# Routed experts of a Mamba and MoE kernel: each slot tile's first expert weights fetched from DRAM into a ring of three groups, in place of a copy picked out of SBUF by VectorE

## The reference

```
def _ffn(xn, rw, W1, W2):
    ms = jnp.mean(xn * xn, axis=-1, keepdims=True)
    h = xn * jax.lax.rsqrt(ms + RMS_EPS) * rw
    return jax.nn.silu(h @ W1) @ W2

gates = jax.nn.softmax(xf @ router_w, axis=-1)           # 8192 tokens, 14 experts
top_v, top_i = jax.lax.top_k(gates, 2)
masked = zeros.at[arange(N)[:, None], top_i].set(top_v)
masked = masked / (masked.sum(-1, keepdims=True) + EPS)
routed = jax.vmap(lambda rw_, W1_, W2_: _ffn(xf, rw_, W1_, W2_))(rms_w, w1, w2)
routed_out = jnp.einsum('end,ne->nd', routed, masked)
shared = the same _ffn for 2 shared experts, summed
return routed_out + shared
```

## Time and profile before

| what | us |
|---|---|
| runs | 765.46, 766.20, 766.67; median 766.2 |
| span of the profiled execution | 769.2 |
| first return of group 0 on POOL | 481.1 |
| return of group 22 begins | 659.5 |
| last return (group 35) begins | 749.34 |

### The profile page before, as it was taken

How to read it: one execution, slowest core, us unless ns; L and a number is a source line. 1 busy time by engine, 2 the same in 40 slices (tenths; PEclk the granted TensorE clock), 3 DMA queues, 4 the chain that set the end, 5 groups by cost and what they waited for, 6 DMA issues and landing times.

```text
span 769.2 us, 14716 instructions
## 1 busy us (share of the span) xinstructions
PE 651.3 (85%) x4299; PEld 554.7 (72%) x4299; DVE 596.1 (77%) x1744; ACT 444.7 (58%) x1225; POOL 501.3 (65%) x545
## 2 busy tenths in 40 slices
PE   5987798999999999999999997965988878767830
PEld 4765576788888888888888886854987768656720
DVE  4999999999999999999999864427447343698875
ACT  4885688867877876787787543411223111346445
POOL 1144565887797897888888776556655656566561
PEclk9999999999999999999999998878889889997865
DMA  8541111211221121111111055114222236536126
GB/s 305 193 138 42 43 43 41 64 57 55 62 64 62 60 62 50 63 64 60 59 50 62 22 167 192 45 55 101 80 80 77 76 80 172 168 100 205 60 80 218
DMA packets 62638, 70.76 MB, mean 92 GB/s; under 512 B 10335, under 2 KB 45285, under 8 KB 62304
## 3 DMA queue, kind: packets, MB, share of 16 engines
q1 hardware_dynamic: 41568, 47.70, 19.6%
q0 software_dynamic: 8608, 16.87, 6.5%
q10 hardware_dynamic: 12384, 5.26, 2.9%
HBM read 48.55 MB, written 23.01 MB: 93 GB/s over the span
## 4 chain that ended last, share of the span: by engine, by line
PE 60%; DVE 13%; issue 12%; ACT 7%; another core or an unknown queue 4%; ACTq 2%; DMA 1%; DVEq 0%; SPq 0%
PE bank L745 7%; PE bank L817 6%; PE bank L826 6%; PE bank L884 6%; PE bank L770 5%; PE bank L800 5%; DVE xbcT_area L1155 3%; PE bank L881 3%; PE bank L871 3%; PE bank L833 3%; PE bank L785 3%; PE bank L888 2%; DVE decay_area L1163 2%; ACT x L933 2%
## 5 line engine op out<-in xcount | busy, mean ns | idle before, releaser
L623 POOL DMA_INDIRECT returned<-xT,slots_in x141 | 142.1, 1008 | 107.6 <-DVE xT L1453 67.3
L669 POOL DMA_INDIRECT dispatched<-rows,row_u x128 | 143.7, 1123 | 33.9 <-issue 31.8
L745 PE MATMUL bank<-xT 128*128 128x128 f32 x564 | 92.0, 316 | 43.4 <-issue 24.9
L1155 DVE SCALAR_TENSOR_TENSOR xbcT_area<-raw,conv_w,xbcT_area 128x512 f32<-128x512 f32 x162 | 123.9, 766 | 2.9 <-ACT xbcT_area L999 2.9
L745 PEld LDWEIGHTS bank<-xT 128*128 128x128 f32 x564 | 82.7, 226 | 50.7 <-issue 42.4
L944 ACT ACTIVATE raw<-bank 128x512 f32<-128x512 f32 (+1 forms) x71 | 39.8, 590 | 126.9 <-remote 61.5
L661 POOL TENSOR_TENSOR state_kept<-state,whole 128x256 f32<-128x256 f32 x56 | 72.1, 1288 | 59.0 <-DVE state L1181 49.1
L1453 DVE COPY xT<-bank 128x512 f32<-128x512 f32 (+1 forms) x36 | 24.3, 676 | 90.5 <-remote 72.8
L770 PE MATMUL bank<-xbcT_area,raw 128*128 x564 | 83.4, 308 | 4.7 <-issue 4.6
L1163 DVE TENSOR_TENSOR_SCAN decay_area<-decay_area,ident_heads 128x512 f32<-128x512 f32 x64 | 85.0, 1329 | 0.0
L770 PEld LDWEIGHTS bank<-xbcT_area,raw 128*128 128x128 f32 x564 | 79.6, 224 | 7.0 <-issue 7.0
(11 more groups left out here) (228 smaller groups left out, 1497.0 us busy)
## 6 DMA issues: line engine op xcount, KB each, us to landing
decay_area<-decay_rows SPq DMA_DIRECT2D x64, 256.0 KB
slots_in<-dispatched ACTq DMA_DIRECT2D x77, 64.5 KB
hid<-returned SPq DMA_DIRECT2D x18, 256.0 KB
slots_in<-dispatched SPq DMA_DIRECT2D x64, 64.5 KB
xT<-xT_dram SPq DMA_DIRECT2D x8, 512.0 KB, 7.9
x<-x_dram SPq DMA_DIRECT2D x8, 512.0 KB, 7.8
out_dram<-x SPq DMA_DIRECT2D x16, 256.0 KB
xT<-returned SPq DMA_DIRECT2D x14, 256.0 KB
```

The lines of the kernel that those rows point to most:

```text
L623: e.indirect_dma_start(returned, bass.IndirectOffsetOnAxis(ap=slots_in[sb_][:, n, D:ROW].bitcast(U32), axis=0), slots_out[b][:, n * P:(n + ...
L669: e.indirect_dma_start(dispatched, bass.IndirectOffsetOnAxis(ap=row_u[t % 2][:, m:m + 1], axis=0), rows[t % 3][:, k, c4, :], None).then_in ...
L745: mm = e.matmul(bank[:, off:off + P], w1_now[b][:, k * P:(k + 1) * P], slotsT[gr % len(slotsT)][:, n % 4 * P:(n % 4 + 1) * P], start=True, ...
L1155: e.scalar_tensor_tensor(o, r[:, n:n + W], conv_w[:, k, TAPS - 1 - n:TAPS - n], o, ALU.mult, ALU.add).then_inc(S["conv"])
```

## The change

`w1_routed` and the picks go. SP fetches, for each of the 141 slot tiles, the 128 x 256 block of its expert from the weights in DRAM (rows of 1 KB, 128 KB each) into `w1_now`, a ring of three groups that lies in the same area. The multiplication by `rms_w` moves to the turned slots: in place of one copy of 128 x 512, DVE has four `tensor_scalar` of 128 x 128 from PSUM to `slotsT`, each with the expert's column of `rms_w`, and each releases its own tile. The experts' numbers come as packed words, four to a word of 16 bits: one read of 12 registers (groups 0 to 11) and one of 24 (the others) on SP, PE and DVE; every tile's expert is a shift and a mask of such a register. For that, three steps are added to each of the two tables on DVE, and the words go from SBUF to DRAM and back as one row, the early ones on ACT's queue, the late ones on SP's. The late part of the tables (`run(later)`) starts one step of the loop earlier.

```
-            experts = []
+            packed = []
-                if gr == 1:
-                    on.wait_ge("mix", NC)
-                    e.dma_start(w1_routed, w1_v[:, 0:NR]).then_inc(S["w1r_loaded"], 16)
+            def load_w1(gr):
+                b = gr % W1_GROUPS
+                on.wait_ge("mix", NC)
+                if gr >= W1_GROUPS:
+                    on.wait_ge("routed_hidden", pairs_of(gr - W1_GROUPS)[-1] + 1)
+                for n in slot_tiles(gr):
+                    expert = expert_of(on, ET.SP, packed, gr, n % 4)
+                    e.dma_start(w1_now[:, b, n % 4, :], w1_v[:, bass.ds(expert, 1), :].rearrange("p o f -> p (o f)")).then_inc(S[f"w1_now{b}"], 16)
...
+            def expert_of(on, engine, packed, gr, j):
+            if gr in (0, EARLY_GROUPS) and j == 0:
+                row, n = (packed_row_early, 2 * TPE) if gr == 0 else (packed_row_late, 2 * TP)
+                on.wait_ge("packed_early" if gr == 0 else "packed_late", 16)
+                packed[:] = regs_of(engine, row, 0, n, 16 ** 4 - 1)
+            word = packed[gr if gr < EARLY_GROUPS else gr - EARLY_GROUPS]
+            return nc.s_assert_within((word >> 4 * j) & 15, 0, NR - 1, ...)
...
+                    e.dma_start(packed_late_d, packed_late).then_inc(S["packed_late_out"], 16)
+                    on.wait_ge("packed_late_out", 16)
+                    e.dma_start(packed_row_late, packed_late_d.rearrange("a b -> (a b)").unsqueeze(0)).then_inc(S["packed_late"], 16)
+                if gr >= W1_GROUPS + W1_LEAD:
+                    load_w1(gr - W1_LEAD)
                 if gr < LOADED_BY_ACT:
                     slots_free(on, gr)
                     if gr % 2 == 0:
                         first_rows = rows_of(ET.SP, gr)
                     load_slots(e, gr, first_rows)
+                if gr < W1_GROUPS:
+                    load_w1(gr)
...
             def routed_hidden(n2):
+                on.wait_ge(f"w1_now{gr % W1_GROUPS}", 16 * tiles_upto(gr, W1_GROUPS))
-                    on.wait_ge("w1_picked", n + 1)
-                    on.wait_ge("slots_turned", gr + 1)
+                    on.wait_ge("slots_turned", n + 1)
...
             def turned(gr):
-                e.tensor_copy(slotsT[gr % len(slotsT)][:, cols], dve_ring.bank("slotsT", gr)[:, cols]).then_inc(S["slots_turned"])
-            def pick_w1(gr):
-                if gr % 2 == 0:
-                    experts[:] = experts_of(on, ET.DVE, gr)
-                    e.tensor_scalar(w1_now[n % len(w1_now)], w1_routed[:, bass.ds(experts[n % 8], 1), :].rearrange("p o f -> p (o f)"), rms_w[:, bass.ds(experts[n % 8], 1)], None, ALU.mult).then_inc(S["w1_picked"])
+                    expert = expert_of(on, ET.DVE, packed, gr, n % 4)
+                    e.tensor_scalar(slotsT[gr % len(slotsT)][:, cols], dve_ring.bank("slotsT", gr)[:, cols], rms_w[:, bass.ds(expert, 1)], None, ALU.mult).then_inc(S["slots_turned"])
```

More of the change, by code:

```diff
@@ L342, in mamba_moe @@
         slotsT = [carve(W) for _ in range(3)]
-        w1_now = [carve(HB * P) for _ in range(8)]
         gexp = carve(NC * NR).rearrange("p (c r) -> p c r", c=NC)
@@ L374, in mamba_moe @@
         rows_a, full_a, base_a, end_a, row_base_a = (carve(NR) for _ in range(5))
-        t_expert_a, t_row_a = (carve(8)[0:TPE, :] for _ in range(2))
+        t_expert_a, t_row_a, in_places_a = (carve(8)[0:TPE, :] for _ in range(3))
         carve, _ = carver(x_third[:].rearrange("p n i -> p (n i)"))
@@ L379, in mamba_moe @@
         seg_sum = carve(SEGS)
-        in_any, t_segment, t_wrap, t_row = (carve(8)[0:TP, :] for _ in range(4))
+        in_any, t_segment, t_wrap, t_row, in_places = (carve(8)[0:TP, :] for _ in range(5))
         lower = y_carried[:, 0:NR * NR].rearrange("p (a b) -> p a b", a=NR)
@@ L427, in regs_of @@
             return vals
[L429 to L435, removed]
+        def expert_of(on, engine, packed, gr, j):
[4 more added lines that the diff above has]
+            word = packed[gr if gr < EARLY_GROUPS else gr - EARLY_GROUPS]
+            return nc.s_assert_within((word >> 4 * j) & 15, 0, NR - 1, skip_runtime_bounds_check_because="worked out from counts")
         def slots_free(on, gr):
@@ L550, in sync_program @@
                     pick(m)
+            for gr in range(GROUPS - W1_LEAD, GROUPS):
+                load_w1(gr)
             stored = 0
@@ L766, in routed_group @@
                     n2, j = n // 2, n % 4
+                    expert = expert_of(on, ET.PE, packed, gr, j)
                     on.wait_ge("routed_silu", n2 + 1)
@@ L1315, in early_table @@
                 yield
+                step(e.scalar_tensor_tensor(by_place(in_places_a), by_place(t_expert_a), float(NR - 1), places[0:TPE], ALU.min, ALU.mult))
+                yield
+                on.wait_ge("early_table", 24)
+                step(e.tensor_reduce(t_row_a[:, 0:2], by_place(in_places_a), AX.X, ALU.add))
+                yield
+                on.wait_ge("early_table", 25)
+                step(e.tensor_copy(packed_early, t_row_a[:, 0:2]))
+                yield
                 step(e.tensor_scalar(seg_row[:, 0], early_of[:], float(P), None, ALU.mult))
@@ L1392, in tables @@
                 assert experts_made == TABLE_EXPERTS, experts_made
+                after(experts_made)
+                placed = step(e.tensor_tensor(by_place(in_places), by_place(expert_late[:]), places[:], ALU.mult))
+                after(placed)
+                words = step(e.tensor_reduce(t_row[:, 0:2], by_place(in_places), AX.X, ALU.add))
+                after(words)
+                packed_made = step(e.tensor_copy(packed_late, t_row[:, 0:2]))
+                assert packed_made == TABLE_PACKED, packed_made
                 after(inside)
@@ L1399, in tables @@
                 after(rows_in)
+                after(packed_made)
                 row = step(e.tensor_reduce(t_row, is_in, AX.X, ALU.add))
```

61 lines of the change are left out of this document (35 added, 26 removed).

## The result

The changed kernel takes 781.1 us (median of 4 runs, 778.96 to 782.29) against 766.4 us before on the same chip: ratio 1.019, interval 1.016 to 1.022, 14.7 us slower. The forecast was 763 us with a range of 749 to 774. The profiled execution of the changed kernel has a span of 778.2 us, 9.0 us over that of before. A time is about 2 us above its span (780.22 us for the span of 778.2), so the profiled execution of the kernel before, with its span of 769.2, was more than 4 us slower than the median of its runs, not 3.0. Comparisons of stages between these two traces therefore understate the loss by 5.7 us in all (14.7 less 9.0).

The account below looks back on a forecast made before the run. Bounds: POOL's runs of indirect DMAs, with PE's slow single matmuls, in groups 12 to 22; DVE's work in groups 22 to 33. Terms -5.5 - 1 + 3 = -3.5 us: span 765.7, median 763 us, range 749 to 774.

Parts of the forecast that it names:

- The start: Ahead of group 1, SP must have the packed words before loading its slots: +3 us, ends 0 and +6.
- SP's queue later: SP in later groups: eight DMAs and a read, about 4.5 us against a pace of 6.5; cost 0.
- Picks out, scaled turns in: DVE in the tail (groups 22 to 33): 0.60 us saved a group, 7.2 at best; -5.5 us taken.
- There DVE is nearly full with the token sums and norms, so DVE's own work decides: Tail, groups 22 to 33: DVE's work sets the pace, a pair of groups taking 13.6 us.
- TENSOR_LOADs: 18 eight-register reads go on each of DVE and PE: -1 us, ends 0 and -3.6.
- The rival in which the stutters go with the reads: PE's slow single matmuls behind POOL's long runs, groups 2 to 22, go: -25 us, about 741; chance 0.12.
- a rival of +8 to +12 at 0.22: SP falls behind at over 0.8 us a DMA, first weights late from group 7 or 8: 772; chance 0.22.
- Traffic: 18.5 MB more in about 270 us, 68 GB/s on top of 79: taken as nothing.

Follow-up runs that it names:

- r5: Kernel before with its turned copy split into four scaled turns, picks kept as multiplications by 1.0: 725.2 against 718.9 us, ratio 1.008.
- r7_after: Changed kernel, unchanged, on chip B (the kind where the kernel before takes 717 to 719 us): 732.9 against 717.1 us, ratio 1.021.
- r4: Changed kernel without first-weight loads after group 2, packed words kept, outputs not the reference's: 721.9 us, ratio 1.006 against the kernel before.
- r15: r12_mended2 without first-weight loads after group 2, outputs not the reference's, on chip B: ratio 0.9965 against the kernel before.
- r17: r12_mended2 once more, on chip B: 718.3 against 718.1 us for the kernel before, ratio 1.000.
- r19: r15 once more, beside r17 (no first-weight loads after group 2, outputs not the reference's): ratio 0.9966 against the kernel before.
- r6_before: Kernel before, unchanged, profiled on chip B: 718.0 us (one execution).
- r8: Kernel before with the picks moved from DVE to ACT: 725.5 against 717.1 us, ratio 1.010.
- r13: Kernel before with late packed words on PE and DVE, their row 64 bytes into its area: 719.1 against 718.4 us, ratio 1.000.
- r18: Changed kernel with experts of groups 0 to 11 by eight-register reads, late packed words kept, on chip B: 723.2 against 718.1 us, ratio 1.007.
- r2: Changed kernel with experts by eight-register reads everywhere, no packed words: 722.4 against 718.9 us for the kernel before, ratio 1.007.
- r12_mended2: r18's kernel, SP reordered: second weights before group 1's first, late words behind group 12's slots, first weights from group 14 a group earlier; chip A, 1.007.
- r16: r12_mended2 with one DMA of four fixed experts a group for first weights, outputs not the reference's, on chip B: ratio 1.002.

## Why the prediction was wrong

Three terms failed: the start was priced at +3 and the early packed words alone cost 7 to 10 us; SP's queue later was priced at nothing and cost 5 us by its order and 2 by its loads on chip B; the tail was to give 5.5 us back and gave 1.8 on chip B and nothing on chip A.

**Picks out, scaled turns in.** The price of the operations was right: four scaled turns start to start take 1.04 us (r5) for 1.64 us of copy and picks. By the section "Why PSUM operands drop a tier" of "VectorE: DVE Perf Modes" in the Trainium skill an fp32 operand in PSUM holds a VectorE operation to the 1x mode. The trace agrees: half the elements out of PSUM took about as long as all of them within SBUF, 351 against 366 ns. The step that failed is "There DVE is nearly full with the token sums and norms, so DVE's own work decides". DVE had 6.5 us less to do in the tail on chip A and 6.0 on chip B. The tail shrank by 1.8 us on chip B (71.5 to 69.6) and grew by 2.0 us on chip A (659.55 to 736.81 before, 666.56 to 745.78 after). The freed time became waits before the copy of the result, 3.9 to 12.3 us on chip A, where no late weights stand in the tail; on chip B one late load of 3.45 us (r7_after) is part of it. Where no first weights are late in the tail (r4, r15, r17, r19, all on chip B) it is 2.0 to 3.6 us shorter than in r6_before, for 5.0 to 6.4 us less work on DVE. The granted clock of that stretch is higher too, 0.87 to 0.94 against 0.86, so not even all of this need be DVE's work; no run separates the two. A busy share of 85% was not enough to call DVE the bound. That the loop DVE, PE, ACT, PE, DVE is the bound instead is argued from these waits; r8 shows ACT's part in it. Term -5.5, measured +2.0 on the chip of the forecast, from one trace of each.

**TENSOR_LOADs.** Term -1, measured 0 for the 12 late reads (r13). The longer reads that came instead were forecast at 1.0 and 2.3 us and took 0.8 to 1.2 and 1.4 to 1.7 us in the changed kernel. The rival in which the stutters go with the reads is dead: the changed kernel has none of the 36 and keeps the stutters on A; the kernel before has all and no stutter on B.

**The start.** Term +3, ends 0 and +6. Measured +6.4 us at group 0 and 2.3 us more by group 3 on B; +5.1 at group 0 on A. With the early words gone the whole kernel wins 10 us on B (r7 against r18) and 7 on A. The mechanism was right and the term mis-sized. I priced the words' way by a DMA's landing, while the DMA out leaves only at 454.35 and the DMA in stands on ACT behind a step of the loop (5.5 us from out to in); group 1's slots were forecast 8 us late at the queue and were 11.4. The reason given for their slow issue before, two loads of 1.8 MB, does not hold either: the second left behind them, at 456.95. I also gave back part of the delay as absorbed by PE's idle time; on B all later groups carried it. The second weights, behind eight loads of first weights on SP, were seen in the order rows but not priced. They show once the early words are gone, with 2.50 us at the first `down` in r2; in the changed kernel itself PE waits 0 to 1.2 us there.

**SP's queue later.** The term was 0: "no cost in the steady state", with a rival of +8 to +12 at 0.22. On B groups 3 to 12 lose 6.3 us, the largest loss of one stage beside the start; on A PE waits 7.2 us for weights. The rival had the place right (groups 8 to 12, behind fills and late words). Its trigger, SP crawling at over 0.8 us a DMA, was seen on A (four loads in 4.3 us) but isn't needed: on B SP takes 0.6 us a load and the weights are late all the same, since their load waits in order behind slots, fills, the words' wait and, at group 24, the first pick of returned rows. The falls of the clock behind such waits, up to 3.0 us behind one, were not in the rival's price. What is shown for order rather than speed is r17 against r18: same loads, another order, 5 us.

**Traffic.** The term was 0; traffic and issues together cost 2 us once the order is mended (r17 against r19, 0.3%).

**The sum on chip B**, in ratios: changed kernel 1.021; early words away 1.007; SP's order mended 1.000; loads away 0.997. So 10 us are the early words, 5 us the order, 2 us the loads, and what is left, turns and late words, is 2.5 us faster than before. The last three ran beside each other; the first ran on another chip of the same kind. The parts add only in this sequence: r4 shows the loads worth 11 us while SP starts late.

**Open.** On chip A r12_mended2 stays 0.7% slower where r17, the same kernel, is even on B. Late weights do not account for it: PE waits for them once in the whole trace of r12, for 1.62 us.

```profile
586.91 3.00 PE L783 MATMUL bank<-xT,decay_area 128*128 128x128 f32 x16 [1.62 <-DMA decay_area<-w_dram]
```

Against the trace of before, it loses 2.3 us in groups 3 to 12, 2.2 in groups 12 to 22 and 0.8 in the tail, where r17 gains. r15 and r16 did not run on A, so the cause is not shown. No version beat the kernel before with the reference's outputs.

## What to carry to other kernels

A load that is cheap in bytes and issues is dear by its place: before moving work to an idle DMA queue, list for each wait on that queue what will stand behind it, and price those, not the mean rate. A busy share of 85% doesn't make an engine the bound; add a little work to it, see in the trace that it was really added (in r5 it was not), and see how much of it reaches the end before spending anything to take work away. A value that many engines need as registers should come from a table that they can read when it is made; its round trip through DRAM took 5.5 us between its two halves here, the time of the program steps around them, and not that of a landing.

## What the runs showed of the hardware

- The same program takes 717 to 719 us on some chips and 766 to 769 us on others. On the slower ones PE issues single matmuls a microsecond or so apart in the second half of a long run of indirect DMAs on POOL (rows 3 to 5, 1.04 us idle before one); on the others POOL runs at 1.28 us a DMA through ten groups. What differs between the chips is not shown.
- A read of 24 registers took 1.6 to 1.8 us on PE and DVE and 1.4 to 1.5 us on SP from a row 64 bytes into its area, and 5.5 (DVE) and 6.2 us (PE) from one 8 bytes in.
- Four loads of 128x256 with a register's offset took mostly 2.35 to 2.4 us of SP's queue on chip B (r7_after); on chip A they took 2.35 to 2.50 us at the start and 3.7 to 4.4 us between 557 and 585 us.
- Behind a wait of PE of 4.00 us the granted clock was 0.50 for 4 us, and 16 passes took 3.78 us instead of 1.95; behind one of 2.75 us, on another chip, they took 2.05 us.
